# The first feed-forward of a six-layer Perceiver kernel: norm, weight turns and logits in one block, the shared expert's gate and up in one product, routing weights in halves

## The chip, the cores and the metric

One core of a Trainium2 chip runs the whole program: six layers, one launch, everything in f32 where it matters here. The metric is the device time of the launch in microseconds, the median of several executions. TensorE is the matrix engine, VectorE (DVE), ScalarE (ACT) and GpSimd (POOL) are the elementwise ones, SyncE (SP) issues the DMAs. SBUF has 128 partitions; PSUM has 8 banks of 128 x 512 f32, and TensorE writes only there.

## The reference, cut to what matters

The residual stream x has 4096 tokens (128 sequences of 32) of 128 features. The third of the six layers is a mixture of experts:

```
h      = layernorm(x)                                  # 4096 x 128
scores = sigmoid(h @ gate_w.T)                         # 16 experts
choice = scores + e_bias                               # 4 groups of 4 experts
         keep the 2 groups with the largest sum of their top two; of these take the 4 best experts
weight = scores[chosen] / (sum + 1e-20) * 2.5
g, u   = h @ gate_proj[e].T, h @ up_proj[e].T          # each expert 64 wide, all 16 are computed
y      = sum over e of weight[e] * (silu(g) * u) @ down_proj[e].T
y     += (silu(h @ shared_gate.T) * (h @ shared_up.T)) @ shared_down.T
x      = x + y
```

## The kernel before, in words

`perceiver_kernel` calls one function a layer; each opens a block in which every engine has its own program, and engines wait for each other by semaphores. A block ends when all engines have ended. The layer of this change is `phase_ffn0` (line 1478). x lies in SBUF as X, 32 tiles of 128 tokens, with the tile statistics made by the layer before.

**Norm.** `phase_norm` (line 165) is a block of its own. VectorE works out mean and 1/sqrt(variance) in a chain of small steps (lines 228 to 242), with one square root on ScalarE (line 256). Then come eight groups of four tiles: VectorE normalises three tiles (line 185), ScalarE one (line 189), TensorE turns the four (line 290) and ScalarE copies the result to XNT (line 268), the features on the partitions. SyncE loads the weights meanwhile (lines 1524 to 1531).

**Main block, start.** TensorE turns the router's weights and the first half of gate_proj, makes the 16 logits of each tile of tokens as 32 products whose moving operand has 16 columns (line 1603; in f32 each product is two instructions), then turns the other expert weights. ScalarE copies what was turned (line 1640) and makes the sigmoid (line 1651).

**Experts.** Two experts (2 x 64) fill the 128 rows of one product, so 8 units hold the 16 experts and the ninth the shared expert; the tokens go in 8 chunks of 512. Unit n of chunk c is `gates(c, a)`, n = 9c + a: a gate product (line 1580) and an up product (line 1583), each 128 x 512. ScalarE makes the Silu of the first (line 1645), VectorE multiplies it by the second into I (`product`, line 1678), GpSimd multiplies units 0 to 7 in place by the routing weights (line 1562), and `down(c)` (line 1592, 36 products of 128 columns, 72 instructions) adds up all nine units for four tiles. VectorE adds the result to X (`finished`, lines 1713 and 1717). The ninth unit's gate and up weights have 64 columns of use each; the other 64 are zeros (ST), so that it too is two full products. I has 4 slots of a chunk each, LAG is 3: TensorE makes units of chunks 0 to 3, then `down(0)`, units of chunk 4, `down(1)` and so on. The gate of unit n waits for Silu n - 2, its up for product n - 2.

**Routing weights.** VectorE finds the experts in a chain of dependent steps (lines 1694 to 1756), and `link` puts one `product()` between them whenever steps worth 4 units of weight have gone by (`room`; a step over all 16 experts counts 3, a small one 1). TensorE turns the result RW behind unit 29 (chunk 3, a = 2, line 1627), ScalarE copies it, SyncE writes it to DRAM (line 1539) and reads it back spread over the partitions as RWB, two reads of 1 MB a chunk (line 1546), each to 64 partitions; RWB has two buffers. GpSimd waits for both reads of a chunk before its first multiplication.

## Time and profile before

| | us |
|---|---|
| median of 3 runs | 2444.99 (2444.36 to 2445.66) |
| the profiled execution's own time | 2440.65 |
| its span, first to last instruction | 2438.7 |
| the layer of the change, in the span | 683.6 to 928.4 |
| TensorE busy in the span | 2083.5 (85%) |
| mean granted TensorE clock | 0.929 of full speed (2.4 GHz) |

One execution is profiled; times of instructions are counted from the start of its span. Busy time is not bound to matter: what counts is the chain of waits that sets the end of the stage. The rows come further down.

### The profile page before, as it was taken

How to read it: one execution, taken by the hardware profiler on the slowest of the kernel's cores; microseconds unless marked ns; L12 is line 12 of the kernel's file. 1: busy time of each engine (PE TensorE's matmuls, PEld its weight loads, DVE VectorE, ACT ScalarE, POOL GpSimd, SP SyncE). 2: the span in 40 equal slices, each digit the busy share in tenths (PEclk: the TensorE clock that was granted, in tenths of full speed). 3: DMA queues.
4: the chain of work that ended last, by engine and by line, in shares of the span. 5: the costliest groups of instructions: out<-in, count | busy, mean ns of one | idle time of the engine just before them, and what ended most of it. 6: DMA issues, size and time to landing. Idle time of an engine off the chain costs nothing. (4 is left out here: it accounts for less than half of the span.)

```text
span 2438.7 us, 77682 instructions
## 1 busy us (share of the span) xinstructions
PE 2083.5 (85%) x25732; PEld 1603.5 (66%) x25771; DVE 1634.8 (67%) x5601; ACT 1427.0 (59%) x3597; POOL 457.9 (19%) x1078
## 2 busy tenths in 40 slices
PE   5999999997988998999999999996556025699999
PEld 3878888875763677999999999995134013444454
DVE  4777777776755235877777787786989877631311
ACT  4888888886743115655555555555677577532322
POOL 2555555552300840000000000000000030000000
PEclk9999999998979999999999999997988555899999
DMA  3222222220012824565556556552000000100000
GB/s 90 81 76 79 75 77 73 77 70 4 0 29 60 164 58 114 120 129 122 106 121 131 109 109 131 120 109 70 0 1 0 0 2 3 49 5 5 9 4 13
DMA packets 266731, 158.07 MB, mean 65 GB/s; under 512 B 40560, under 2 KB 256512, under 8 KB 266240
## 3 DMA queue, kind: packets, MB, share of 16 engines
q1 hardware_dynamic: 266624, 156.65, 27.9%
q8 instruction: 66, 1.08, 0.2%
q14 instruction: 41, 0.34, 0.1%
HBM read 135.34 MB, written 21.23 MB: 64 GB/s over the span
## 5 line engine op out<-in xcount | busy, mean ns | idle before, releaser
L1195 ACT ACTIVATE c_PR<-c_PR,c_nmx 128x257 f32<-128x257 f32 x512 | 252.8, 496 | 69.8 <-DVE c_nmx L1242 69.8
L1238 DVE CUSTOM_DVE_ANT_0 c_PR<-c_b,c_MB 128x257 f32<-128x257 f32 x512 | 195.1, 424 | 125.4 <-PE c_b L1120 118.5
L684 ACT ACTIVATE a_PR<-a_SM,a_nmx 128x257 f32<-128x257 f32 x512 | 253.3, 499 | 4.1 <-POOL a_XL L459 3.6
L1131 PE MATMUL c_b<-c_PT,c_C 32*128 32x128 f32 x8192 | 238.8, 272 | 3.7 <-ACT c_QP L1188 2.1
L1131 PEld LDWEIGHTS c_b<-c_PT,c_C 32*128 32x128 f32 x8192 | 232.3, 187 | 7.9 <-issue 4.3
L1120 PE MATMUL c_b<-c_cT,c_QP 128*128 128x257 f32 x1024 | 230.5, 383 | 0.8 <-ACT c_QP L1188 0.8
L731 DVE CUSTOM_DVE_ANT_0 a_SM<-a_bs,a_MB 128x257 f32<-128x257 f32 x512 | 188.0, 423 | 60.4 <-PE a_bs L552 33.5
L1120 PEld LDWEIGHTS c_b<-c_cT,c_QP 128*128 128x128 f32 x1024 | 191.9, 190 | 31.2 <-issue 2.8
L1255 DVE STREAM_TRANSPOSE c_PT<-c_PR 128x256 f32<-128x256 f32 x512 | 181.4, 412 | 0.0
L1200 ACT ACTIVATE c_OT<-c_b 128x512 f32<-128x512 f32 x128 | 76.4, 597 | 169.0 <-PE c_b L1131 169.0
L1088 POOL TENSOR_TENSOR c_XL<-quarter,c_PR 128x16 f32<-128x16 f32 x128 | 27.6, 216 | 660.8 <-DVE c_PR L1250 660.8
L1250 DVE TENSOR_SCALAR c_PR<-c_PR,c_rden 128x257 f32<-128x257 f32 x512 | 146.3, 351 | 4.5
L2693 ACT ACTIVATE g_A<-g_b,g_S 128x512 f32<-128x512 f32 x64 | 44.0, 687 | 160.8 <-PE g_b L2614 160.7
L562 PE MATMUL a_bp<-ident,a_PR 128*128 128x128 f32 x1024 | 134.5, 274 | 1.7 <-ACT a_PR L684 1.4
L2813 DVE TENSOR_TENSOR g_YS<-g_b,g_s 128x512 f32<-128x512 f32 x8 | 5.5, 692 | 183.7 <-PE g_b L2668 183.7
L1150 PEld LDWEIGHTS c_b<-c_B,c_OT 128*128 128x128 f32 x1024 | 116.7, 192 | 16.1 <-DVE c_mx L1238 13.7
L2369 PE MATMUL d_bv<-d_WQ,d_HQ 128*128 128x512 bf16 x33 | 20.7, 633 | 124.8 <-PEq L2209 96.2
L1150 PE MATMUL c_b<-c_B,c_OT 128*128 128x128 f32 x1024 | 122.8, 278 | 4.6 <-DVE c_mx L1238 3.1
L1105 PE MATMUL c_b<-c_XNT,c_A 128*128 (+1 forms) x1024 | 122.1, 278 | 1.6 <-POOL c_VB L1094 1.6
L1188 ACT ACTIVATE c_QP<-c_b 128x512 f32<-128x512 f32 x128 | 75.7, 596 | 76.4 <-PE c_b L1105 76.4
L562 PEld LDWEIGHTS a_bp<-ident,a_PR 128*128 128x128 f32 x1024 | 117.0, 144 | 3.0 <-ACT a_PR L684 3.0
L1105 PEld LDWEIGHTS c_b<-c_XNT,c_A 128*128 128x128 f32 x1024 | 117.0, 192 | 2.5 <-POOL c_VB L1094 2.5
(496 smaller groups left out, 4804.1 us busy)
## 6 DMA issues: line engine op xcount, KB each, us to landing
c_C<-in_ctx_dram SPq DMA_DIRECT2D x512, 128.0 KB, 3.1
a_C<-in_ctx_dram SPq DMA_DIRECT2D x128, 128.0 KB, 2.1
ctxT_dram<-a_cT SPq DMA_DIRECT2D x128, 128.0 KB, 1.8
f_RWB<-f_rw_dram SPq DMA_DIRECT2D x16, 1024.0 KB, 13.5
c_cT<-ctxT_dram SPq DMA_DIRECT2D x128, 128.0 KB, 3.2
a_MK<-in_mask_Bx1xSxS_bk_dram SPq DMA_DIRECT2D x128, 32.1 KB, 1.9
X<-in_x_dram SPq DMA_DIRECT2D x4, 512.0 KB, 6.4
g_h<-in_L_ffn_h_w_dram SPq DMA_DIRECT2D x2, 1024.0 KB, 6.9
```

The lines of the kernel that those rows point to most:

```text
L562: last = nc.tensor.transpose(b_pt[pair][:, (2 * k + c) * P:(2 * k + c + 1) * P], PR[:, par, 2 * pair + k, c * P:(c + 1) * P], sh.ident[:, :])
L684: nc.scalar.activation(PR[:, 1 - par, hg, :], SM[:, 1 - par, hg, :], ACT.Exp, bias=nmx[:, 1 - par, hg:hg + 1], accum_out=den[:, 1 - par, h ...
L731: nc.vector.tensor_tensor_reduce(SM[:, par, hg, :], b_s[hg][:, 0:SK], MB[:, par, :], 1.0, NEG1, ALU.add, ALU.max, mx[:, par, hg:hg + 1]).t ...
L1105: last = nc.tensor.matmul(banks[:, c, i * P:(i + 1) * P], A[:, 4 * c + i, :], sh.XNT[:, ds(tile * P, P)], start=True, stop=True)
L1120: nc.tensor.matmul(banks[:, hg, 0:SK], QP[:, s.r, b, 4 * hg:4 * hg + 4, :], cT[:, buf, :], start=True, stop=True).then_inc(s_ps, 1)
L1131: last = nc.tensor.matmul(banks[:, h, 0:P], C[rows, b, kb, :], PT[rows, b, kb, :, :], start=(kb == 0), stop=(kb == NKB - 1), tile_position ...
L1150: nc.tensor.matmul(second[:, 0, 0:D], OT[:, par, h, :, :], BH[:, h, :], start=(h == 0), stop=False)
L1195: nc.scalar.activation(PR[:, b, hg, :], PR[:, b, hg, :], ACT.Exp, bias=nmx[:, b, hg:hg + 1], scale=SCALE, accum_out=den[:, b, hg:hg + 1]). ...
L1200: nc.scalar.activation(OT[:, par, :, b, :].rearrange("p (a h) q -> p h a q", h=4), banks[:, :, 0:P].rearrange("p h (a q) -> p h a q", a=4) ...
L1238: nc.vector.tensor_tensor_reduce(PR[:, b, hg, :], banks[:, hg, 0:SK], MB[:, :], 1.0, NEG1, ALU.add, ALU.max, mx[:, b, hg:hg + 1]).then_inc ...
L1250: nc.vector.tensor_scalar(PR[:, b, hg, :], PR[:, b, hg, :], rden[:, b, hg:hg + 1], None, ALU.mult).then_inc(n_ok, 1)
L1255: nc.vector.transpose(PT[:, b, :, hg, :], PR[:, b, hg, 0:LAST]).then_inc(t_ok, 1)
```

## The change

The norm's block goes: `phase_ffn0` has one block, and norm, weight turns and logits are interleaved by hand in each engine's order. The logits are made with the router's weights as the stationary operand, one product of 512 columns for each group of four tiles, and turned back in pieces of 16 rows into the same PSUM bank as before; half of the groups are copied by ScalarE, half by VectorE, and so are the turned expert weights. The shared expert's gate and up weights are turned together, so that one product gives the gate in partitions 0 to 63 and the up in 64 to 127; ScalarE writes the Silu to partitions 64 to 127, and the product and the down weights use these. The routing weights' turn stands behind unit 25 in place of 29, `room` begins at -8, `down(c)` follows the first two units of chunk c + 4 in place of the end of chunk c + 3, RW has another order, and each chunk's weights are read back in four DMAs of 512 KB, two for units 0 to 3 and two for units 4 to 7, for which GpSimd waits in turn.

```diff
--- before.py
+++ after.py
-        ST = sb("f_ST", [D, 2, P])
+        ST = sb("f_ST", [D, P])
...
-        sg, su = sb("f_sg", [FI, D]), sb("f_su", [FI, D])
-        sd = sb("f_sd", [P, FI])
+        sgu, sd = sb("f_sgu", [P, D]), sb("f_sd", [D, P])
...
-        RW = sb("f_RW", [P, 4, E_, NT // 4])
+        RW = sb("f_RW", [P, NC, 2, KE, 4])
...
+        LT = I[0:E_, LAG, 0:NC, :]
...
+            sp.dma_start(sgu[0:FI, :], sg_w).then_inc(s_in, 16)
+            sp.dma_start(sgu[FI:P, :], su_w).then_inc(s_in, 16)
...
-        phase_norm(nc, sh, "f_n_", loads, bk[0:2])
...
                 wait(sp, w_ok, KE * (c - 1))
-                rows = rw_dram[c // 2].rearrange("(a o) t k -> o a (t k)", o=2)
-                for o in range(2):
-                    sp.dma_start(RWB[FI * o:FI * o + FI, c % 2, :, :],
-                                 bcast(rows[o, :, CT * (c % 2):CT * (c % 2) + CT], 0, FI)).then_inc(rwb_in[c % 2], 16)
+                for h in range(2):
+                    for o in range(2):
+                        first = 64 * (c % 2) + 32 * o + 16 * h
+                        rows = rw_dram[c // 2, first:first + 16, :].rearrange("p k -> (p k)")
+                        sp.dma_start(RWB[FI * o:FI * o + FI, c % 2, 4 * h:4 * h + 4, :].rearrange("p a k -> p (a k)"),
+                                     bcast(rows, 0, FI)).then_inc(rwb_in[c % 2][h], 16)
...
+            clear_retired(pool)
...
+            nc.gpsimd.memset(sd[:, 0:FI], 0.0).then_inc(sd0_ok, 1)
+            nc.gpsimd.memset(I[0:FI, :, KE, :], 0.0).then_inc(zero_ok, 1)
             for c in range(NC):
-                pool.wait_ge(rwb_in[c % 2], 32 * (c // 2 + 1))
                 for a in range(KE):
+                    if a % 4 == 0:
+                        pool.wait_ge(rwb_in[c % 2][a // 4], 32 * (c // 2 + 1))
                     pool.wait_ge(i_ok, NA * c + a + 1)
                     nc.gpsimd.tensor_tensor(I[:, c % (LAG + 1), a, :], I[:, c % (LAG + 1), a, :], RWB[:, c % 2, a, :],
...
+            def rows(g):
+                pe.wait_ge(normed_v, g + 1)
+                pe.wait_ge(normed_a, g + 1)
+                wait(pe, xt_ev, g - 1)
+                for r in range(4):
+                    last = nc.tensor.transpose(tp[g % 2][:, r * P:(r + 1) * P], xn[:, g % 2, r, :], sh.ident[:, :])
+                last.then_inc(turned, 1)
+
+            def logits(g):
+                pe.wait_ge(xt_ev, g + 1)
+                wait(pe, lt_a if g % 2 else lt_v, g // 2)
+                nc.tensor.matmul(b_y[g % 2][0:E_, :], gateT[:, :], sh.XNT[:, g * CT:(g + 1) * CT],
+                                 start=True, stop=True).then_inc(lt_ps, 1)
+
+            def back(g):
+                pe.wait_ge(lt_a if g % 2 else lt_v, g // 2 + 1)
+                for r in range(4):
+                    t = 4 * g + r
+                    last = nc.tensor.transpose(b_l[:, t * E_:(t + 1) * E_], LT[:, g, r * P:(r + 1) * P],
+                                               sh.ident[0:E_, 0:E_])
+                return last
...
+                if a == 1:
+                    wait(pe, i_ok, n - 1)
+                nc.tensor.matmul(b_g[n % 2][:, :], GT[:, a * P:(a + 1) * P] if a < KE else ST[:, :], x,
                                  start=True, stop=True).then_inc(g_ps, 1)
-                wait(pe, i_ok, n - 1)
-                nc.tensor.matmul(b_u[n % 2][:, :], UT[:, a * P:(a + 1) * P] if a < KE else ST[:, 1, :], x,
-                                 start=True, stop=True).then_inc(u_ps, 1)
...
+            weights(b_t, [gw[:, :]], tw_ps)
+            rows(0)
+            pe.wait_ge(g_in, 16)
+            weights(bk[2], [gp[:, a, :] for a in range(4)], tw_ps)
+            rows(1)
+            pe.wait_ge(tw_a, 1)
+            logits(0)
+            pe.wait_ge(u_in, 16)
+            weights(bk[3], [up[:, a, :] for a in range(4)], tw_ps)
+            rows(2)
+            logits(1)
+            back(0)
+            weights(b_t, [gp[:, 4 + a, :] for a in range(4)], tw_ps)
+            rows(3)
+            logits(2)
+            back(1)
+            pe.wait_ge(tw_v, 1)
+            weights(bk[2], [up[:, 4 + a, :] for a in range(4)], tw_ps)
+            rows(4)
+            logits(3)
+            back(2)
             pe.wait_ge(s_in, 32)
-            turn(b_t, [sg[:, :], su[:, :]])
-            pe.wait_ge(t_ev, 5)
-            for c in range(NC + LAG):
-                if c < NC:
-                    for a in range(NA):
-                        if c == 0 and a == KE:
-                            pe.wait_ge(t_ev, 6)
-                            pe.wait_ge(st0_ok, 1)
-                        gates(c, a)
-                        if c == 1 and a < 2:
-                            pe.wait_ge(d_in, 32)
-                            turn(b_y[a], down_weights(a))
-                        if c == 1 and a == 2:
-                            turn(b_t, [sd[:, :]])
-                        if c == LAG and a == 2:
-                            pe.wait_ge(rw_ok, 1)
-                            for q in range(4):
-                                last = nc.tensor.transpose(b_l[:, q * P:(q + 1) * P],
-                                                           RW[:, q, :, :].rearrange("p e t -> p (e t)"), sh.ident[:, :])
-                            last.then_inc(rw_ps, 1)
-                if c >= LAG:
-                    if c == LAG:
-                        pe.wait_ge(t_ev, 9)
-                        pe.wait_ge(dt0_ok, 1)
-                    down(c - LAG)
+            pe.wait_ge(tw_a, 2)
+            weights(bk[3], [sgu[:, :]], tw_ps)
+            rows(5)
+            logits(4)
+            back(3)
+            rows(6)
+            logits(5)
+            back(4)
+            rows(7)
+            logits(6)
+            back(5)
+            pe.wait_ge(tw_v, 3)
+            pe.wait_ge(xt_ev, 7)
+            gates(0, 0)
+            logits(7)
+            back(6)
+            pe.wait_ge(tw_a, 3)
+            gates(0, 1)
+            back(7).then_inc(l_ps, 1)
+            for c in range(NC):
+                for a in range(2 if c == 0 else 0, NA):
+                    gates(c, a)
+                    if c == 1 and a < 2:
+                        pe.wait_ge(d_in, 32)
+                        weights(b_y[a], [dn[:, 8 * a + 2 * k:8 * a + 2 * k + 2, :].rearrange("p a b -> p (a b)")
+                                         for k in range(4)], dn_ps)
+                    if c == 1 and a == 2:
+                        pe.wait_ge(sd0_ok, 1)
+                        weights(b_t, [sd[:, :]], dn_ps)
+                    if c == LAG - 1 and a == KE - 1:
+                        pe.wait_ge(rw_ok, 1)
+                        for q in range(4):
+                            last = nc.tensor.transpose(b_l[:, q * P:(q + 1) * P],
+                                                       RW[:, 2 * q:2 * q + 2, :, :, :].rearrange("p c o a t -> p (c o a t)"),
+                                                       sh.ident[:, :])
+                        last.then_inc(rw_ps, 1)
+                    if c > LAG and a == 1:
+                        if c == LAG + 1:
+                            pe.wait_ge(dn_ev, 3)
+                            pe.wait_ge(zero_ok, 1)
+                        down(c - LAG - 1)
+            for c in range(NC - LAG - 1, NC):
+                down(c)
...
+                if n % NA < KE:
+                    nc.scalar.activation(SG[:, n % 2, :], b_g[n % 2][:, :], ACT.Silu).then_inc(g_ok, 1)
+                else:
+                    nc.scalar.activation(SG[FI:P, n % 2, :], b_g[n % 2][0:FI, :], ACT.Silu).then_inc(g_ok, 1)
...
+            nc.scalar.activation(warm[:, 0:1], sh.ident[:, 0:1], ACT.Sqrt)
+            act.wait_ge(var_ok, 1)
+            nc.scalar.activation(rstd, var, ACT.Sqrt).then_inc(std, 1)
+            nc.scalar.activation(warm[:, 1:2], sh.ident[:, 0:1], ACT.Sigmoid)
+            weights(0, gateT[:, :], b_t[:, 0:E_])
+            act.wait_ge(ready, 1)
+            normalised(0)
+            normalised(1)
+            copied(0)
+            weights(2, UT[:, 0:512], bk[3][:, :])
+            normalised(2)
+            copied(1)
+            normalised(3)
+            copied(2)
+            logits(1)
+            normalised(4)
+            copied(3)
+            normalised(5)
+            copied(4)
+            logits(3)
+            weights(5, ST[:, :], bk[3][:, 0:P])
+            normalised(6)
+            copied(5)
+            normalised(7)
+            copied(6)
+            logits(5)
+            copied(7)
+            logits(7)
...
-                if n == NA * LAG + 2:
+                    down_weights(2, DT[:, KE, :], b_t[:, 0:P])
+                if n == NA * LAG - 2:
...
-            n = room = made = 0
+            n = made = 0
+            room = -8
...
+            normalised(0)
+            normalised(1)
+            weights(1, GT[:, 0:512], bk[2][:, :])
+            logits(0)
+            normalised(2)
+            normalised(3)
+            weights(3, GT[:, 512:FE], b_t[:, :])
+            logits(2)
+            normalised(4)
+            weights(4, UT[:, 512:FE], bk[2][:, :])
+            normalised(5)
+            logits(4)
+            normalised(6)
+            normalised(7)
+            logits(6)
...
+            for o in range(2):
+                last = nc.vector.tensor_tensor(
+                    RW[:, :, o, :, :].rearrange("p c a t -> p c t a"),
+                    SEL[:, :, :].rearrange("p (c t) (a o) -> p c t a o", t=4, o=2)[:, :, :, :, o],
+                    bcast(tot[:, 1, :].rearrange("p (c t) -> p c t", t=4), 3, KE), ALU.mult)
+            last.then_inc(rw_ok, 1)
+            while made < NA * (LAG + 1):
                 product()
-            for c in range(LAG, NC + LAG):
-                while made < min(NA * (c + 1), NA * NC):
+            for c in range(LAG + 1, NC):
+                while made < NA * c + 2:
                     product()
-                finished(c - LAG)
+                finished(c - LAG - 1)
+                while made < NA * (c + 1):
+                    product()
+            for c in range(NC - LAG - 1, NC):
+                finished(c)
```

(`weights` in TensorE's program is the old `turn` with the semaphore as an argument; the norm's small steps on VectorE are those of `phase_norm`, and `normalised`, `copied` and `logits` on the other two engines wait for the turn or product, then normalise a tile or copy a bank.)

## Rows read from the trace of the kernel before

**Rows 1.** Timeline, 683 to 718: start us, us, engine, line, count [idle before]
```profile
687.28 1.83 DVE L185 TENSOR_SCALAR f_n_xn<-X,f_n_small 128x128 f32 x6 [0.29 <-issue]
688.25 2.03 PE L290 MATMUL f_b<-ident,f_n_xn 128*128 128x128 f32 x8 [6.19 <-DVE f_n_xn L185]
...
699.94 13.84 PE L1603 MATMUL f_b<-f_gateT,f_XNT 128*128 128x16 f32 x64 [0.28 <-ACT f_gateT L1640]
713.82 0.60 ACT L1651 ACTIVATE f_S<-f_b 128x512 f32<-128x512 f32 x1 [13.44 <-PE f_b L1603]
717.11 1.12 PE L1580 MATMUL f_b<-f_XNT,f_GT 128*128 128x512 f32 x2 [0.31 <-ACT f_UT L1640]
717.24 1.28 ACT L1656 ACT_TABLE_LOAD   x1
```
**Rows 2.** Windows: stretch, PE PEld DVE ACT POOL busy, clock, DMA share, GB/s
```profile
686.50:688.00 1.50, 0.00 (x0) 0.00 (x0) 1.14 (x6) 0.90 (x2) 0.00 (x0) 0.50 1.16 335
688.00:698.00 10.00, 8.25 (x32) 5.73 (x32) 6.48 (x22) 7.08 (x14) 0.00 (x0) 0.50 0.53 95
700.00:713.50 13.50, 13.50 (x64) 13.50 (x65) 0.00 (x0) 0.38 (x1) 0.00 (x0) 0.50 0.00 0
716.50:718.00 1.50, 1.19 (x4) 0.62 (x5) 0.00 (x0) 1.48 (x3) 0.00 (x0) 0.95 0.00 0
784.50:786.00 1.50, 0.00 (x0) 0.00 (x0) 0.00 (x0) 0.00 (x0) 0.00 (x0) 0.64 0.99 199
850.00:870.00 20.00, 20.00 (x85) 11.87 (x84) 7.07 (x13) 4.78 (x8) 14.36 (x13) 1.00 1.02 190
938.00:940.00 2.00, 2.00 (x23) 1.49 (x21) 0.36 (x1) 1.23 (x3) 0.00 (x0) 0.87 0.04 8
```
**Rows 3.** Timeline of VectorE, the routing chain
```profile
714.52 0.69 DVE L1694 TENSOR_TENSOR f_C<-f_S,f_eb 128x512 f32<-128x512 f32 x1 [18.27 <-ACT f_S L1651]
...
719.25 0.69 DVE L1678 TENSOR_TENSOR f_I<-f_SG,f_b 128x512 f32<-128x512 f32 x1 [3.62 <-ACT f_SG L1645]
...
755.92 1.09 DVE L1756 TENSOR_TENSOR f_RW<-f_SEL,f_tot 128x512 f32<-128x512 f32 x1
```
**Rows 4.** Timeline of TensorE, the routing weights' turn and the first down product
```profile
770.56 0.60 PE L1627 MATMUL f_b<-ident,f_RW 128*128 128x128 f32 x4
...
780.44 1.02 PE L1583 MATMUL f_b<-f_XNT,f_ST 128*128 128x512 f32 x2
798.61 9.89 PE L1592 MATMUL f_b<-f_DT,f_I 128*128 128x128 f32 x72 [17.15 <-POOL f_I L1562]
808.33 1.02 PE L1580 MATMUL f_b<-f_XNT,f_GT 128*128 128x512 f32 x2
809.19 1.02 PE L1583 MATMUL f_b<-f_XNT,f_UT 128*128 128x512 f32 x2
```
**Rows 5.** Timelines of SyncE and GpSimd; the reads of RWB: ns min/median/max
```profile
771.82 0.37 SPq L1539 DMA_DIRECT2D f_rw_dram<-f_TM  x1
774.11 85.17 SPq L1546 DMA_DIRECT2D f_RWB<-f_rw_dram  x16
...
L1546 SPq DMA_DIRECT2D f_RWB<-f_rw_dram x16: 573/636/2115, 774.1 to 858.6; - x16
...
788.55 9.80 POOL L1562 TENSOR_TENSOR f_I<-f_I,f_RWB 128x512 f32<-128x512 f32 x8 [89.11 <-DMA f_RWB<-f_rw_dram]
...
863.63 9.85 POOL L1562 TENSOR_TENSOR f_I<-f_I,f_RWB 128x512 f32<-128x512 f32 x8 [5.64 <-DMA f_RWB<-f_rw_dram]
```
**Rows 6.** Timeline of TensorE, the last four down products
```profile
894.25 32.32 PE L1592 MATMUL f_b<-f_DT,f_I 128*128 128x128 f32 x288
```
**Rows 7.** DMA issues, 680 to 900: KB, us to landing (issued at 683.98)
```profile
f_gp<-in_L_ffn_gate_proj_dram SPq DMA_DIRECT2D x1, 512.0 KB, 4.2
```
**Rows 8.** Timeline of TensorE, the next stage's first turns
```profile
932.53 1.97 PE L848 MATMUL c_b<-ident,c_wq 128*128 128x128 f32 x8 [5.96 <-DMA c_wq<-in_L_xattn_W_Q_dram]
```
**Rows 9.** Timeline of GpSimd, a memset of 256 columns
```profile
953.01 0.31 POOL L1094 MEMSET c_VB<- 64x256 f32 x1
```

More of the change, by code:

```diff
@@ L1515, in phase_ffn0 @@
[L1515 to L1517 removed]
+        rw_dram = nc.dram_tensor("f_rw_dram", (4, P, P), F32, kind="Internal").ap()
+        total, mean, diff, dsq, msq, var, rstd, half, shift = (small[:, i, :] for i in range(9))
+        gw_in, g_in, u_in, s_in, d_in, e_in = (sem("f_" + n) for n in ("gw_in", "g_in", "u_in", "s_in", "d_in", "e_in"))
@@ L1566, in _, with weights @@
         def _(pe):
-            def turn(bank, srcs):
+            def weights(bank, srcs, done):
                 for a, src in enumerate(srcs):
```

147 lines of the change are left out of this document (86 added, 61 removed).

## The prediction

> **What bounds the kernel now.** I read the page first: the span is 2438.7 us and the change touches one stage of it, from 683.6 to 926.6 us, so only that stage's own chain counts. The timeline then cuts it into four stretches. (a) From 687.28, when VectorE begins to normalise, to 717.11, when the first expert product starts, TensorE turns the normalised rows, then makes 64 logit products in 13.8 us, then turns the expert weights [rows 1], at half clock [rows 2]. (b) From 714.5 to 757.0 VectorE works out the routing weights: C at 714.52, the last product at 755.92 plus 1.09 [rows 3]. It puts 20 expert products between these steps, and waits 3.62 us for the first. (c) The weights are turned on TensorE only at 770.56, behind unit 29 of the gate and up products; they go to DRAM at 771.82, the first copy back is issued at 774.11, GpSimd starts at 788.55 [rows 4, 5]. TensorE has nothing left from 781.5 (780.44 plus 1.02) until the first down product at 798.61. (d) From there TensorE never stops: the last four down products, 288 instructions, take 32.32 us to 926.57 [rows 6].
>
> So the end of the stage is: start of the first down product plus TensorE's work behind it. A 512-column product in f32 (two instructions) takes 0.86 us at full clock, 808.33 to 809.19 [rows 4]; a chunk of 9 units is 18 of them, 15.45 us; a down product of 72 instructions 32.32 / 4, 8.04 us start to start. 798.61 + 4 x 15.45 + 8 x 8.04 + 1.7 (the first down product took 808.33 - 798.61 = 9.7 us, its clock being low after the idle time) = 926.4, and the trace has 926.57.
>
> **What the change does to each term.** *Shared expert as one product.* 17 products a chunk, not 18: 17 x 0.858 = 14.59 us, 0.86 us saved a chunk. Scalar and vector work keep their widths along the free axis (512), so their times stand.
>
> *Down products two units into the chunk.* The first one now comes after 38 units, not 36, and what stands behind it is 4 x 14.59 - 2 x 1.72 + 64.3 = 119.2 us, against 126.1. The slots of I free as before; VectorE makes two products and then adds the chunk to X. The next gate and up pair waits about 0.1 us for the first of these; I cost it at nothing, hidden by the 0.86 us gate product in front of it.
>
> *Start, one block.* The vector steps up to 687.28 stay, and the square-root table loads beside them as it did. The first rows can be turned at 688.25 as now [rows 1]; the gate weights land 683.98 + 4.2 = 688.2 [rows 7]. TensorE then has, up to the first half of the up weights, 16 transposes at 0.215 us (8 took 1.97 us at 932.53 [rows 8]) and one logit product of 512 columns, 1.72 us at half clock (twice 0.86, an estimate): 5.1 us, to 693.4. Does the clock rise then? In the next stage, whose norm is mixed with weight turns in the same way, it rose between 938 and 940, some 6 us after its first transpose [rows 2, 8]. I take full clock from 693.4. Then 33 transposes x 0.108, 6 logit products x 0.86 and 24 small turns of 16 columns: for these the nearest rows are the 64 logit instructions, 0.215 us each at half clock [rows 1], and the down product's 0.112 at full [rows 6]. I take 0.112. Sum 3.6 + 5.15 + 2.7 = 11.4 us.
> To this come waits that the new orders make. ScalarE normalises its tile of group 2 behind the copy of the up weights, which waits for their turn: TensorE stands 1.4 us. VectorE copies logits 2 and 4 before it normalises groups 4 and 6 (a copy of 0.6 and three tiles of 0.3 us each, 6 in 1.83 [rows 1]): 0.8 and 1.25 us. So the first expert product starts at 693.4 + 11.4 + 3.5 = 708.4 (bounds: 705 with no waits, 719.8 at half clock), 8.7 us sooner than 717.11.
>
> *Routing chain.* The logits now end behind two expert units: 708.4 + 2 x 1.72 + 0.86 + 8 x 0.112 = 713.6. Sigmoid 713.8, C 714.5: **no sooner than now**. The chain itself was 42.5 us. The 3.62 us wait goes, since the first product is due after 12 weight units instead of 4; 18 products, not 20, stand in it (2 x 0.6 less); the last step becomes two of half the size (+0.1, between +0 and +1.1). End 757.0 - 3.6 - 1.2 + 0.1 = 752.3. The price is that TensorE stands about 4.4 us near 715, for the Silu table (1.28 us [rows 1]) and for the first product at 718.3. It costs nothing as long as VectorE's chain is the bound; nothing else queues behind it.
>
> *Turn of the weights.* It stands behind unit 25. TensorE can't be further, at the chain's end, than VectorE's products let it: up product 20 waits for product 18, done at 752.9. Then 0.86 + 5 x 1.72 us: turned from 762.4, **8.2 us sooner** than 770.56.
>
> *Halves.* Write issued 1.25 us after (771.82 - 770.56), first read 2.3 us later: 765.95. Now the first chunk's two reads take 14.4 us to GpSimd's start, then 8 multiplications 9.8 us [rows 5]. In halves the second half is there after the same 14.4 us, and only 4 multiplications (4.9 us) stand behind it, the first four being done beside the load: 780.35 + 4.9 + 0.26 = **785.5** for the first down product, 13.1 us sooner than 798.61. SP issues 32 reads instead of 16 at 0.64 us [rows 5], 2.5 us a chunk, beside transfers of about 12.5 us. TensorE comes there at 762.4 + 0.43 (four turns) + 0.86 + 14.59 + 3.43 = 781.7, so 3.8 us idle instead of 17.
>
> *Clock.* In the idle time after 781.5 the slice 784.5 to 786 has a mean clock of 0.64 [rows 2]: it fell in it. My idle time of 3.8 us is about as long as that took, and it may fall or not: cost 0 to 1.7 us, and I take 1.7.
>
> *Small things.* GpSimd clears the old semaphores and sets 2048 columns of I to zero: 8 x 0.31 us by the nearest row [rows 9], needed only at 785, so free. It runs beside VectorE's first norm steps; if it holds them up, by at most that 2.5 us.
>
> **Sum.** 785.5 + 119.2 + 1.7 = 906.4 against 926.4: 20 us less. The profiled execution took 2440.65 us, so 2420.6; the median of the runs shown is 4.3 us above it: **2425**. A difference under 0.2% (4.9 us) can hardly be told from none here.
>
> **Rivals.**
> *Cold start* (chance 0.12). The clock was at 0.50 through the whole of the old norm (688 to 698), though TensorE was busy for 82% of it, and through the 64 logit products (700 to 713.5) with TensorE always busy; it rose only behind the weight turns, in 716.5 to 718 [rows 2]. If it stays there, 11.4 us become 22.8, the first product comes at 719.8 and the chain starts 11 us or more later: gain 5 to 10 us, 2437. For it: ScalarE and VectorE leave gaps. Against: the next stage's rise with the same mix.
>
> *Faster copies* (0.12). The reads now have lines of 8 KB in place of 2 KB, and alternate between the partition halves. Now they run at 190 GB/s with a DMA share of 1.02, while weight loads reach 335 [rows 2]. If they gain a third, 14.4 us become 10.8, and TensorE finds all ready when it comes at 781.7: gain 20 + 3.8 + 1.7 = 25.5, 2419. Against: both use the same source lines for 64 partitions, and that doesn't change.
>
> *Halves that cost* (0.10). The transfers are half as large, twice as many. If the per-chunk load goes from 12.5 us (863.63 - 788.55 over 6 chunks [rows 5]) to 15.6, the first down product is 3.6 us later: gain 16, 2429. If it goes over 18.4 us, GpSimd's stream sets the end: 765.95 + 8 x 18.4 + 4.9 + 8.3 = 926.4, and from there on the kernel is **slower**, by 8 us for each us more; at 20 us a chunk it is 2458 (chance of that 0.04, within the 0.10). Against: single loads of 512 KB are the quick ones above, so size isn't what limits the reads. The Trainium skill, "DMA: Bandwidth & Descriptors", section Bandwidth, advises batching to 1 MiB or more and has smaller transfers at a lower share of the peak; by its table a 512 KB transfer would run at roughly four fifths of the 1 MB rate (estimate), which is this rival's 15.6 us. The trace disagrees so far: 335 GB/s for 512 KB, 190 for 1 MB.
>
> *The early weights don't come early* (0.06). The idle time near 715 lets the clock fall, units 2 to 5 run at 3.4 us, and VectorE's chain waits for them: up to 5 us more, gain 15, 2430.
>
> **Numbers.** The forecast's own case has 0.60, with 2420 to 2428 from its bounds (+3 for a stretched last step and GpSimd's zeros, -5 for no waits and no clock loss). To hold 8 in 10 the range goes down to the faster copies, 2418, and up towards the cold start, 2436. Faster by over 0.2%: all but the slow half of the cold start and the slow loads: 0.92; within 0.2% 0.04; slower 0.04.
>
> **What would show it.** Right: first expert product near 708, C near 714.5, turn of the weights near 762, first down product near 785, chunk period 22.6 us in place of 23.5, stage end near 906. The first four multiplications of chunk 0 should start about 6 us before the second four. Wrong: half clock beyond 700, a chunk load over 15 us, or a down product that waits for GpSimd after the first.

## The result and the profile after

| | before | after |
|---|---|---|
| median | 2444.68 us (2442.03 to 2445.66, 4 runs) | 2422.57 us (2419.85 to 2422.83, 4 runs) |
| ratio, with its 95% interval | | 0.9907 (0.9894 to 0.992) |
| profiled execution, its span | 2440.65, 2438.7 | 2419.85, 2418.1 |
| the layer (the stage), from its first weight load to the next layer's | 244.86 | 227.44 |

The kernel is 22.1 us faster by the medians. The two profiled spans differ by 20.6 us, of which 17.4 lie in the layer; the other 3.2 come from layers that the change does not touch, and are spread between executions. Everything below is about the 17.4.

The timeline of TensorE, after, answers to [rows 1, 4, 6]: start us, us, engine, line, count, idle before.
```profile
689.00 1.12 PE L1582 MATMUL f_b<-ident,f_xn 128*128 128x128 f32 x4 [3.97 <-DVE f_xn L1773]
...
694.72 0.63 PE L1582 MATMUL f_b<-ident,f_xn 128*128 128x128 f32 x4 [1.11 <-DVE f_xn L1773]
695.27 1.03 PE L1588 MATMUL f_b<-f_XNT,f_gateT 128*16 128x512 f32 x2
696.24 0.42 PE L1595 MATMUL f_b<-ident,f_I 16*128 16x16 f32 x4
696.58 0.66 PE L1574 MATMUL f_b<-ident,f_gp 128*128 128x128 f32 x4
...
709.13 1.12 PE L1605 MATMUL f_b<-f_XNT,f_GT 128*128 128x512 f32 x2
...
714.27 0.42 PE L1595 MATMUL f_b<-ident,f_I 16*128 16x16 f32 x4
717.38 1.12 PE L1605 MATMUL f_b<-f_XNT,f_GT 128*128 128x512 f32 x2 [2.69 <-ACT f_SG L1714]
720.09 2.08 PE L1609 MATMUL f_b<-f_XNT,f_UT 128*128 128x512 f32 x2 [1.58 <-DVE f_I L1799]
...
764.61 0.60 PE L1678 MATMUL f_b<-ident,f_RW 128*128 128x128 f32 x4
...
786.62 9.90 PE L1618 MATMUL f_b<-f_DT,f_I 128*128 128x128 f32 x72 [2.49 <-POOL f_I L1566]
796.36 1.02 PE L1605 MATMUL f_b<-f_XNT,f_GT 128*128 128x512 f32 x2
797.36 1.13 PE L1609 MATMUL f_b<-f_XNT,f_UT 128*128 128x512 f32 x2
...
834.11 8.20 PE L1618 MATMUL f_b<-f_DT,f_I 128*128 128x128 f32 x72
...
857.01 8.20 PE L1618 MATMUL f_b<-f_DT,f_I 128*128 128x128 f32 x72
...
876.45 32.32 PE L1618 MATMUL f_b<-f_DT,f_I 128*128 128x128 f32 x288
```
The first expert product starts at 709.13 and the weights are turned at 764.61, 6 us sooner than in [rows 4]. The wait for GpSimd before the first down product is 2.49 us in place of 17.15. Two down products stand 22.90 us apart.

The timeline of VectorE, after, answers to [rows 3]:
```profile
685.76 0.19 DVE L1854 SCALAR_TENSOR_TENSOR f_small<-f_small 128x32 f32<-128x32 f32 x1
685.99 1.73 DVE L1855 TENSOR_SCALAR f_small<-f_small 128x32 f32<-128x32 f32 x1
...
715.42 0.69 DVE L1817 TENSOR_TENSOR f_C<-f_S,f_eb 128x512 f32<-128x512 f32 x1 [5.85 <-ACT f_S L1751]
...
751.66 0.69 DVE L1801 TENSOR_TENSOR f_I<-f_SG,f_b 64x512 f32<-64x512 f32 x1
...
753.21 1.08 DVE L1913 TENSOR_TENSOR f_RW<-f_SEL,f_tot 128x256 f32<-128x256 f32 x2
```
The routing chain takes 38.87 us, from 715.42 to 754.29, against 42.5. At its head, line 1855 takes 1.73 us where its neighbours of the same width take 0.19.

The timelines of GpSimd and SyncE, after, answer to [rows 5]:
```profile
685.89 1.80 POOL L1560 MEMSET f_I<- 64x2048 f32 x1
775.38 4.95 POOL L1566 TENSOR_TENSOR f_I<-f_I,f_RWB 128x512 f32<-128x512 f32 x4 [87.69 <-DMA f_RWB<-f_rw_dram]
781.43 54.00 POOL L1566 TENSOR_TENSOR f_I<-f_I,f_RWB 128x512 f32<-128x512 f32 x44 [1.10 <-DMA f_RWB<-f_rw_dram]
...
765.87 0.37 SPq L1542 DMA_DIRECT2D f_rw_dram<-f_TM  x1
768.17 70.13 SPq L1550 DMA_DIRECT2D f_RWB<-f_rw_dram  x32
```
The first half of chunk 0 is multiplied from 775.38, 6.05 us before the second. After that GpSimd makes 44 multiplications without a wait for a load.

Windows, after, as in [rows 2]:
```profile
692.00:693.50 1.50, 1.50 (x6) 0.42 (x4) 0.45 (x1) 0.00 (x0) 0.00 (x0) 0.92 0.00 0
693.50:708.00 14.50, 11.59 (x65) 5.74 (x65) 7.49 (x23) 8.24 (x18) 0.00 (x0) 1.00 0.00 0
719.40:722.60 3.20, 2.52 (x3) 1.17 (x4) 2.99 (x12) 0.60 (x1) 0.00 (x0) 0.52 0.00 0
788.00:791.00 3.00, 3.00 (x16) 3.00 (x16) 0.00 (x0) 0.00 (x0) 3.00 (x3) 0.50 0.95 199
800.00:830.00 30.00, 30.00 (x124) 17.57 (x123) 10.23 (x18) 7.76 (x13) 30.00 (x25) 1.00 1.02 218
```
TensorE's clock rises to 2.4 GHz just behind 692, falls to 1.2 GHz once near 720 and once more inside the first down product. The copies now run at 218 GB/s, against 190.

### The profile page after: what moved, and what is told of

Read it like the earlier page. It is cut to its first block and busy times, and to the rows that moved or that the text cites. A ratio compares the mean times of both kernels' runs of the same rounds, so it can differ in the third digit from the quotient of the medians.

```text
span 2418.1 us, 77577 instructions
## 1 busy us (share of the span) xinstructions
PE 2085.1 (86%) x25738; PEld 1586.2 (66%) x25738; DVE 1639.1 (68%) x5609; ACT 1426.7 (59%) x3599; POOL 459.2 (19%) x1078
## 3 DMA queue, kind: packets, MB, share of 16 engines
q8 instruction: 66, 1.08, 0.2%
## 5 line engine op out<-in xcount | busy, mean ns | idle before, releaser
L2533 PE MATMUL d_bv<-d_WQ,d_HQ 128*128 128x512 bf16 x64 | 33.1, 621 | 112.0 <-PEq L2373 96.0
```

## The experiments

"Stage" is the time from the layer's first weight load to the next layer's; the changed kernel has 227.44. "Turn" and "first down product" are counted from the same start: 81.40 and 103.41. Each kernel had one execution profiled, so that a difference of some tenths of a microsecond between two rows may be chance; the rows marked "again" show how far one kernel repeats. Times of the layer in us, C being the start of the routing chain on VectorE:

| kernel | stage | first expert product | C | turn | first down product |
|---|---|---|---|---|---|
| before | 244.86 | 33.52 | 30.93 | 86.97 | 115.02 |
| before, again (b_again) | 248.09 | 32.87 | 30.29 | 88.66 | 117.03 |
| after | 227.44 | 25.92 | 32.21 | 81.40 | 103.41 |
| after, again (c_again) | 227.62 | 25.94 | 32.23 | 81.44 | 103.59 |
| x1_whole | 233.25 | 26.46 | 32.76 | 82.22 | 109.29 |
| x2_lines | 229.74 | 26.45 | 32.74 | 82.19 | 105.74 |
| x3_extra | 230.28 | 26.52 | 32.81 | 82.29 | 104.50 |
| x4_turn20 | 223.16 | 25.97 | 32.27 | 72.89 | 100.83 |
| y7_turn29 | 232.73 | 26.12 | 32.41 | 87.74 | 108.94 |
| z1_oldstart | 225.11 | 32.73 | 29.98 | 81.95 | 102.71 |
| y1_zeros | 225.44 | 25.09 | 31.38 | 80.99 | 103.04 |
| y2_order | 224.93 | 23.09 | 29.38 | 78.83 | 100.90 |
| y3_room0 | 225.22 | 25.90 | 32.19 | 80.60 | 102.81 |
| y6_best | 215.00 | 23.79 | 24.59 | 64.73 | 92.67 |

Two things in these rows don't come from the edits. In x1_whole, x2_lines and x3_extra TensorE's clock rose 10.1 to 10.3 us into the layer, in the changed kernel 9.1: their first expert product is 0.5 us later and their turn 0.8 to 0.9, and these three are compared from the first read on. And the clock fell in the first down product of some executions and not of others, which is worth 1.6 us of the stage (last section).

**Halves (x1_whole).** Two reads of 1 MB a chunk, one wait.
```diff
-                for h in range(2):
-                    for o in range(2):
-                        first = 64 * (c % 2) + 32 * o + 16 * h
+                for o in range(2):
+                    first = 64 * (c % 2) + 32 * o
...
-                    if a % 4 == 0:
-                        pool.wait_ge(rwb_in[c % 2][a // 4], 32 * (c // 2 + 1))
+                    if a == 0:
+                        pool.wait_ge(rwb_in[c % 2][0], 32 * (c // 2 + 1))
```


> The changed kernel, with the routing weights of a chunk read back in two reads of 1 MB and waited for once, as before the change (the 8 KB lines stay). Theory 1 (halves let four of eight multiplications run beside the load): GpSimd starts when all has landed, 13.3 us after the first read, and needs 9.8 us; the first down product starts 4.9 us later than 786.6 and the stage (first weight load to the next stage's first load, 227.4 us in the changed kernel) is 4.9 us longer, 232.3. Theory 2 (twice as many, half as large reads are slower and eat the gain): whole reads land by more than 2 us sooner and the stage is longer by under 3 us. Theory 3 (the halves do nothing): 227.4.

The first theory's number: from the first read to the first down product it took 23.51 us against 18.45, 5.06 more, the four multiplications (4.95) that no longer run beside the load. The timelines of GpSimd and TensorE:
```profile
781.40 19.62 POOL L1565 TENSOR_TENSOR f_I<-f_I,f_RWB 128x512 f32<-128x512 f32 x16 [94.75 <-DMA f_RWB<-f_rw_dram]
803.84 9.86 POOL L1565 TENSOR_TENSOR f_I<-f_I,f_RWB 128x512 f32<-128x512 f32 x8 [2.83 <-DMA f_RWB<-f_rw_dram]
...
791.46 9.83 PE L1617 MATMUL f_b<-f_DT,f_I 128*128 128x128 f32 x72 [7.55 <-POOL f_I L1565]
```
GpSimd also waits for loads again between chunks, 2.83 us here, but TensorE isn't held by that: the second down product starts 24.52 us after the first, 24.59 in the changed kernel. The stage grew by 5.81 us; the 0.75 beyond the 5.06 lie ahead of the first read.

**Order of the weights in DRAM (x2_lines).** The halves stay; RW and its DRAM tensor have the old order, so that a line read is 2 KB in place of 8.
```diff
-        RW = sb("f_RW", [P, NC, 2, KE, 4])
+        RW = sb("f_RW", [P, 4, E_, NT // 4])
...
-                        first = 64 * (c % 2) + 32 * o + 16 * h
-                        rows = rw_dram[c // 2, first:first + 16, :].rearrange("p k -> (p k)")
+                        rows = rw_dram[c // 2].rearrange("(a o) t k -> o a (t k)", o=2)
...
+                                     bcast(rows[o, 4 * h:4 * h + 4, CT * (c % 2):CT * (c % 2) + CT], 0, FI)
```


> The changed kernel, still in halves, but with the order of the routing weights as before the change, so that a line read is 2 KB and not 8 KB. Theory 1 (the length of a line sets the rate of these reads): the rate falls from about 217 to about 200 GB/s, the second half of the first chunk lands 14.4 us after the first read in place of 13.3, and the stage is 1.1 us longer, 228.5; GpSimd waits for loads again in later chunks. Theory 2 (the 64 partitions of a read, not its lines, set the rate): 227.4 and the same rate.

Read to down product: 19.99 us, 1.54 more; GpSimd starts on the second half of chunk 0 14.81 us after the first read, in place of 13.26. The window of the same 30 us from 770, first of x2_lines:
```profile
770.00:800.00 30.00, 25.97 (x111) 16.46 (x109) 5.97 (x10) 5.96 (x10) 20.52 (x17) 0.94 0.91 198
```
then of the changed kernel:
```profile
770.00:800.00 30.00, 27.51 (x113) 17.02 (x112) 8.49 (x16) 6.56 (x11) 23.52 (x20) 0.94 1.03 219
```
So the new order is worth 1.5 us here, more than the 1.1 expected. My prediction had this as a rival and not as a term.

**The shared expert's product (x3_extra).** One 512-column product into the unused bank is put back into each ninth unit; nobody reads it.
```diff
+                else:
+                    wait(pe, i_ok, n - 1)
+                    nc.tensor.matmul(b_u[n % 2][:, :], ST[:, :], x, start=True, stop=True)
```


> The changed kernel with a second 512-column product in the ninth unit of every chunk, whose result nobody reads (the work that the one product for gate and up took away). Theory 1 (only what stands behind the first down product counts): 4 products of 0.86 us there, 3.4 us; of the four ahead of it, two fall where VectorE is the bound and two shorten TensorE's 2.5 us of waiting for GpSimd; stage 230.9. Theory 2 (TensorE is the bound all along): 8 x 0.86 = 6.9 us, 234.3. Theory 3 (product and Silu are the bound, not TensorE): under 1 us.

As the first theory said, the time from the end of the first down product to the end of the stage grew from 114.29 to 117.67 us: 3.38, four times 0.85. The stage grew by 2.84 only: the first down product came 1.09 us later, and in this execution the clock did not fall in it, 1.63 less.

**The turn's place (y7_turn29, x4_turn20).** Behind unit 29, where it was, and behind unit 20, with ScalarE's copy moved along. The first, then the second:
```diff
-                    if c == LAG - 1 and a == KE - 1:
+                    if c == LAG and a == 2:
...
-                if n == NA * LAG - 2:
+                if n == NA * LAG + 2:
```


> The changed kernel with the turn of the routing weights behind unit 29, its place before the change. Theory 1 (TensorE's order sets when the weights leave): the turn comes 0.86 + 3 x 1.72 = 6.0 us later, at 87.4 us of the stage, the first down product 6.0 us later at 109.4, and the stage is 6.0 us longer, 233.4 (with the clock's fall at the first down product, as in the changed kernel). Theory 2 (the sooner turn is worth nothing once the reads come in halves): under 2 us.

```diff
-                    if c == LAG - 1 and a == KE - 1:
+                    if c == LAG - 1 and a == 2:
...
-                if n == NA * LAG - 2:
+                if n == NA * (LAG - 1) + 2:
```


> The changed kernel with the turn of the routing weights behind unit 20 in place of 25. Theory 1 (the weights were ready at 754.3 and waited 10.3 us for their place in TensorE's order): the turn comes near 755.5, 9 us sooner; TensorE no longer waits for GpSimd before the first down product (2.5 us) and its clock doesn't fall there (1.7 us): stage 4.2 us shorter, 223.2. Theory 2 (the fall of the clock has to do with the down products, not with the wait): 2.5 us shorter, 224.9. Theory 3 (GpSimd and the loads, not TensorE's place, were last): no change.

The timeline of TensorE, of y7_turn29:
```profile
773.37 0.60 PE L1678 MATMUL f_b<-ident,f_RW 128*128 128x128 f32 x4
...
794.57 9.67 PE L1618 MATMUL f_b<-f_DT,f_I 128*128 128x128 f32 x72 [7.71 <-POOL f_I L1566]
```
and of x4_turn20:
```profile
756.60 0.60 PE L1678 MATMUL f_b<-ident,f_RW 128*128 128x128 f32 x4
...
784.54 8.20 PE L1618 MATMUL f_b<-f_DT,f_I 128*128 128x128 f32 x72
```
Four units later costs 5.3 us of the stage, where 6.0 were expected. The turn is 6.3 us later, but the first down product only 5.5, since from read to down product it took 17.39 us in place of 18.45. The four reads of chunk 0 show why. In the changed kernel the fourth landed 3.6 us behind the third, where its neighbours land 2.4 us apart, and in that time a 16 KB packet of the queue that the profile calls instruction held one of the 16 DMA engines for 1.3 us:
```profile
q8 instruction: 1, 0.02, 1.9%
```
(the DMA view of the changed kernel, 777.2 to 781.5: kind, packets, MB, share of the engines). In y7_turn29 that packet went 2.8 us before the first read, all gaps were 2.4 us, and GpSimd never waited for the second half. In each of the nine executions with the same reads in which such a packet went among the first ten reads, exactly one gap is 3.6 to 3.7 us, and the packet began in it or at most 1 us ahead of it. So at equal loads the place would be worth some 1.1 us more, about 6.4 (an estimate from these two executions).

Five units sooner gains 4.3: the turn comes 8.5 us sooner, but the wait had 2.49 us left to lose and the clock 1.7. Then TensorE comes to the first down product and finds everything ready, as the first theory said. The change left these 4 us where a constant in the program put them: the chain had ended at 754.29, and the weights waited 10.3 us for their place in TensorE's order.

**The new start (z1_oldstart).** The norm in its own block again, 64 logit instructions, all copies on ScalarE; everything behind it as changed.
```diff
+        phase_norm(nc, sh, "f_n_", loads, bk[0:2])
+        block = ctx.enter_context(nc.Block())
...
+            for t in range(NT):
+                last = nc.tensor.matmul(b_l[:, t * E_:(t + 1) * E_], sh.XNT[:, t * P:(t + 1) * P], gateT[:, :],
+                                        start=True, stop=True)
```


> The changed kernel with the old start: the norm in a block of its own, then 64 logit instructions of 16 columns and the weight turns, all copies on ScalarE; everything from the first expert unit on as changed. Theory 1 (only the time at which the logits are done counts, since VectorE's routing chain is the bound from there): C comes at 30.9 us of the stage as before the change, 1.3 us sooner than the changed kernel's 32.2, the first expert product 7.6 us later at 33.5, and the stage stays within 1.5 us of 227.4. Theory 2 (the sooner first expert product is what the new start brings): 7.6 us longer, 235.

The first expert product is 6.8 us later, C is 2.2 us sooner, and the turn comes only 0.55 us later: VectorE gets to its first product and waits 2.62 us for it. Its timeline, then GpSimd's:
```profile
720.28 0.69 DVE L1754 TENSOR_TENSOR f_I<-f_SG,f_b 128x512 f32<-128x512 f32 x1 [2.62 <-PE f_b L1611]
...
776.26 19.66 POOL L1568 TENSOR_TENSOR f_I<-f_I,f_RWB 128x512 f32<-128x512 f32 x16 [76.24 <-DMA f_RWB<-f_rw_dram]
```
So at the turn the largest part of the diff, the new start, is worth half a microsecond. This execution's stage is even 2.3 us shorter than the changed kernel's. Of that 1.6 is the clock, which did not fall in its first down product (8.11 us to the next product against 9.74), and 1.2 the reads: no instruction packet fell into those of chunk 0, GpSimd made 16 multiplications without a wait, and from read to down product it took 17.21 us. The half microsecond is one execution's: its clock was at 2.4 GHz from 693 to 699.5, in the old norm and just behind it, where the kernel before had 1.2 from 688 to 698 [rows 2], and at 1.2 again when the first units ran. A new start that is worth nothing, or 1 us, isn't excluded.

**What the start leaves (y1_zeros, y2_order, y3_room0).** GpSimd's zeros wait for the last normalised tile of VectorE; VectorE and ScalarE normalise before they copy logits and weights; `room` begins at 0.
```diff
+            pool.wait_ge(normed_v, 8)
             nc.gpsimd.memset(I[0:FI, :, KE, :], 0.0).then_inc(zero_ok, 1)
```


> The changed kernel with GpSimd's memset of 2048 columns of I moved behind the norm. Theory 1 (the memset holds a VectorE step of the norm: 1.73 us where it takes 0.19): normalising starts 1.5 us sooner, and so do the logits and the stage's end: 225.9. Theory 2 (TensorE's clock rises at the same time whatever it did 1.5 us sooner, and takes part of it back): 226.5 to 227. Theory 3 (the long step has another cause): 227.4.

```diff
-            weights(2, UT[:, 0:512], bk[3][:, :])
             normalised(2)
             copied(1)
             normalised(3)
+            weights(2, UT[:, 0:512], bk[3][:, :])
...
-            logits(0)
             normalised(2)
+            logits(0)
```
(and the same for logits 2 and 4)

> The changed kernel with normalising put ahead of the copies that wait for TensorE: on VectorE groups 2, 4 and 6 before logits 0, 2 and 4, on ScalarE groups 2 and 3 before the up weights. Theory 1 (the three waits of TensorE in the start, 1.1, 0.6 and 1.2 us, come from these copies): first expert product and C 2.9 us sooner, stage 224.5. Theory 2 (other copies are then last, ScalarE's above all): less than half of it.

```diff
-            room = -8
+            room = 0
```


> The changed kernel with room starting at 0 in place of -8, so that VectorE makes its first product after 4 units of weight. Theory 1 (with the turn behind unit 25 the number of products made in the chain counts, not its end): the chain ends 2 us later, but with 20 products made in place of 18, so the turn of the weights comes 1.4 us sooner (2 x 1.72 - 2.0), and the stage is 1.4 us shorter, 226.0; TensorE's clock doesn't fall near 720. Theory 2 (the end of the chain is what counts): 2 us longer, 229.4.

y1_zeros: line 1856, the step that line 1855 had been, is short again. Its timeline of VectorE:
```profile
686.90 0.19 DVE L1855 SCALAR_TENSOR_TENSOR f_small<-f_small 128x32 f32<-128x32 f32 x1
687.12 0.18 DVE L1856 TENSOR_SCALAR f_small<-f_small 128x32 f32<-128x32 f32 x1
```
The 1.5 us shrank to 0.83 at the first expert product and 0.41 at the turn, since the clock did not rise sooner with the work: by the windows of half a microsecond around it, it rose between 692 and 692.5 in the changed kernel and behind 693 in y1_zeros, whose layer begins 1.14 us later, so about 9 us into the layer in both. More of the turns ran at 1.2 GHz, as the second theory had it. The next 0.4 us went when the clock stayed down from 717.4 to 724, in the changed kernel from 719.7 to 722.9, and the first products came late. The stage's 225.44 looks like the first theory's 225.9, but that is luck: 1.6 of its 2.0 us are the clock, which did not fall in the first down product.

y2_order: the three waits of 1.11, 0.60 and 1.20 us are gone, and 2.83 us of that arrive at C and 2.57 at the turn. The same chain, moved, is moved to its end: that is what counts in the start, not when the first expert product runs.

y3_room0: a product is done sooner, the clock doesn't fall near 720 (1.00 over 716 to 724), and the turn comes 0.80 us sooner although the chain ends 1.86 later. So beginning at -8 made the chain shorter and fed TensorE later. The gain is smaller than the 1.4 us expected, since TensorE now waits 1.00 and 1.01 us near the chain's end and the clock falls there instead:
```profile
751.00:754.00 3.00, 3.00 (x5) 1.15 (x4) 2.77 (x5) 0.60 (x1) 0.00 (x0) 0.50 0.00 0
```
Of the 2.2 us by which its stage is shorter, 1.6 are again the clock in the first down product.

**All together (y6_best).** x4_turn20, y1_zeros and y2_order, and all logits ahead of the first two units, so that C need not wait for them:
```diff
             pe.wait_ge(tw_v, 3)
-            pe.wait_ge(xt_ev, 7)
-            gates(0, 0)
             logits(7)
             back(6)
+            back(7).then_inc(l_ps, 1)
             pe.wait_ge(tw_a, 3)
+            gates(0, 0)
             gates(0, 1)
-            back(7).then_inc(l_ps, 1)
```


> Turn behind unit 20, zeros behind the norm, normalising ahead of the copies, and all logits done ahead of the first two expert units, so that VectorE's routing chain starts sooner and the two units fall into TensorE's idle time of 4.4 us behind them. Theory 1 (the parts add up, since each brings the routing chain or the first down product forward): 223.2 of x4_turn20, less 2.5, less 0.4, less 3.1 for the chain's sooner start, 217.1; against the changed kernel 10.3 us, a ratio to the kernel before of 0.987. Theory 2 (the first product, Silu's table and the units themselves are late then): no more than 1 us from the last part, 219.5.

Its timeline of TensorE:
```profile
749.41 0.60 PE L1678 MATMUL f_b<-ident,f_RW 128*128 128x128 f32 x4
...
777.35 8.20 PE L1619 MATMUL f_b<-f_DT,f_I 128*128 128x128 f32 x72
```
Median 2410.18 us (2409.24 to 2410.87, 4 runs), ratio to before 0.9855 (0.984 to 0.9871); the changed kernel, timed beside it, has 2421.56 and 0.9901 (0.9887 to 0.9915). It beats both. The stage is 12.4 us shorter than the changed kernel's, where the parts add up to 10.3; its clock stayed at 2.4 GHz from 694 to 777 (1.00), and what else the 2.1 us are no run shows.

**The same kernels again (c_again, b_again).** No edit.

> The changed kernel once more, on the chip and against the kernel before of y6_best. Stage 227.4, or 225.8 where TensorE's clock doesn't fall at the first down product (it fell in two of four runs with a gap of 2.5 to 2.7 us before it). Theory 1 (that fall is chance): ratio to the kernel before 0.990 to 0.993. If y6_best's parts add up, it is 8 to 11 us slower than that one.

> The kernel before, once more, to see how far a stage's length repeats. If it does, the stage takes 244.9 us within 1 us and what is left of the span 2193.8 within 2 or 3 us. Theory 1 (the change does nothing outside its stage): the rest is in the range that the changed kernels show, 2190.7 to 2196.2. Theory 2 (later stages gain too): the rest is over 2196.

The changed kernel repeats within 0.2 us of the stage. The kernel before does not: b_again's stage is 3.2 us longer, where I expected 1 us at most, while the rest of its span is 2193.4 us, the 2193.8 of the first execution. Its timeline of VectorE, beside the 3.62 us of [rows 3]:
```profile
720.72 0.69 DVE L1678 TENSOR_TENSOR f_I<-f_SG,f_b 128x512 f32<-128x512 f32 x1 [5.36 <-PE f_b L1583]
```
and its windows:
```profile
716.00:720.00 4.00, 3.72 (x7) 1.80 (x7) 0.00 (x0) 2.85 (x5) 0.00 (x0) 0.50 0.00 0
```
Its clock rose near 721.6, 37.6 us into the layer, in [rows 2] 33.1 us into it, so the first units ran at 1.2 GHz and VectorE waited 1.74 us longer for the first product. The first down product took another 1.2 us more (10.93 to the next product, not 9.72). By the mean of the two executions of each kernel the stage fell from 246.5 to 227.5 by 18.9 us.

## Why the prediction was right, and where its terms were off

Predicted 2425.0 (2418 to 2436), measured 2422.57: the likeliest case came true. The sum was made for the profiled execution, 2420.6, which took 2419.85. But the stage itself was predicted 20 us shorter and is 17.4 shorter, so the sum was partly saved by the 3.2 us outside the stage, which no term stands for: that is luck. So is some of the median: I put it 4.3 us above the profiled execution, as before the change, and it is 2.7 above. Of the 22.1 us between the medians, some 19 are the stage's by the repeated profiles; the other 3 are no more than the runs of the kernel before differ among themselves (2442.03 to 2445.66).

- **Start.** From the stage's start, predicted 24.8 and measured 25.92. The clock rose just behind 692, not at 693.4; the cold start of the rivals came in none of the eleven executions that have the new start (a rise 9.0 to 10.3 us into the layer). The three waits came nearly as predicted, 1.11, 0.60 and 1.20 us for 1.4, 0.8 and 1.25. Three terms were too small. The step that GpSimd's zeros hold was named ("if it holds them up, by at most that 2.5 us") and costed at nothing; it is 1.5 us. A logit product of 512 columns takes 0.97 us to the next instruction, 695.27 to 696.24, not 0.86, 0.7 us for six. And a turn of a normalised tile takes 0.14 us to the next, not 0.108, 0.8 us for the 24 of them; the small turns, 0.086 us in place of 0.112, gave 0.6 back.
- **C "no sooner than now".** Right as a statement, and 1.3 us off in size: 32.21 from the start, predicted 30.9, in the kernel before 30.93. y6_best shows that this was mostly a choice of order: C can be at 24.59, of which y2_order alone has 2.8 us and y1_zeros 0.8.
- **The chain.** Predicted 37.8 us, measured 38.87. The wait of 3.62 us went, as predicted. The split last step cost nothing: 1.08 us for both, as one did in [rows 3]. The missing 1.1 us are in the timeline of VectorE. The shared expert's products have only 64 partitions (line 1801), and around each of the two in the chain 0.12 us are lost twice, ahead of it (0.72 us from the step before to the product, where others have 0.60 or 0.61) and behind it (0.72 for 0.60): 0.5 us. VectorE waits 0.40 us for TensorE after its clock had fallen near 720. And the two products that no longer stand in the chain saved 1.04 us, not 1.2: without one between them, two dependent steps start 0.33 us apart, with one the product starts 0.21 us after the first.
- **The early weights.** The rival with 0.06 came half true: TensorE stood near 715 and its clock fell (0.52 in 719.4 to 722.6). It cost 0.40 us of VectorE's chain, not 5, because only one product was late for it.
- **The turn.** Chain's end plus 10.3 us, predicted 10.1. Its time, 764.61 for 762.4, is late by the start and the chain. y7_turn29 prices the new place at 5.3 us.
- **Halves.** Read to the second half: 13.26 us, predicted 14.4. This term was mis-sized in our favour by 1.1 us: I kept the old rate, and the copies run at 218 GB/s. Without the instruction packet it would have been 1.2 us less still: the fourth read landed after 11.9 us in z1_oldstart and 12.1 in y7_turn29. The four multiplications off the path are 5.06 us (x1_whole), predicted 4.9.
- **First down product.** 786.62 for 785.5, idle before 2.49 us for 3.8, and its clock fell as assumed: 9.74 us for 8.04 plus 1.7.
- **Behind it.** 122.15 us (to 876.45 + 32.32) for 119.2 + 1.7. "I cost it at nothing" failed for the pair behind a down product: the up product does wait for VectorE's first product, as the prediction said, and is not hidden. From the waits of the changed kernel, 817 to 822 (PEld is the load of the stationary operand; us in all, times, longest):
```profile
PEld f_b L1609 <- DVE f_I L1799: 0.8, 1, 0.8
```
The gate product takes 1.00 us to the next, the up product 0.96, where both took 0.86 in the kernel before (831.82, 832.68, 833.54). Per chunk 22.90 us for 22.63, four times 0.27. The saved product itself is 3.38 us for 4 x 0.86 = 3.44.
- **Faster copies**, as a rival, had a third more rate. They got 15%. The Trainium skill, "SBUF — State Buffer", section "Door 1: The DMA port swizzle", states about 218 GB/s as what a transfer to partitions 0 to 63 can reach, half the ports of one to all 128. The trace agrees within a few per cent: 218 GB/s over 30 us, 225 over the 11 us from 770, and the single loads to 128 partitions in [rows 2] have 335. With that page of the Trainium skill this rival would have been smaller: by its figure 2 MB take 9.6 us per chunk (an estimate). The reads land 2.4 us apart, four of them a chunk.
- **Halves that cost** fell. In x1_whole, with reads of 1 MB and the same 8 KB lines, the 2 MB of chunk 0 reach GpSimd 13.45 us after the first read; in halves 13.26. Between 770 and 781 it moved 207 GB/s, the changed kernel 225. The rule of the Trainium skill, "DMA: Bandwidth & Descriptors", section Bandwidth, to batch to 1 MiB or more, which its table has for 128 partitions, doesn't hold for these reads.

Where the 17.4 us came from, each from the run that takes one part away: the turn's place 5.3, halves 5.1, longer lines 1.5, one product less in each of the four chunks behind the first down product 3.4, the new start 0.5. That is 15.8, or about 17 with the 6.4 for the turn's place at equal loads. The two units made ahead of the first down product take 3.4 us from behind it and cost 1.1 us in slower pairs; no run took them away alone, and the parts overlap where TensorE comes too late itself, so the sum isn't exact.

## What to carry to other kernels

Follow a result to the instruction that waits for it, and ask what stands before that instruction in its engine's order: here the weights lay ready for 10 us behind five units that could wait, and moving one `if` gained as much as splitting all transfers, while a rewritten start that ran 7 us ahead was worth 0.5 in the one execution that shows it. When a transfer feeds a chain of equal pieces, let the first pieces be released before the last have landed. And profile a kernel twice: the stage of the kernel before moved by 3.2 us with the times at which its clock rose, more than several of the terms in the sum, and nearly 3 us of an edit's price can be the clock (1.6) and one packet of instructions (1.2).

## What the runs showed of the hardware that was not expected

- A GpSimd memset, which reads nothing, holds a VectorE step of 32 columns until it ends: 1.73 us in place of 0.18 (y1_zeros). The step has one input from SBUF; the one before it, at 685.76 and with two, ran in 0.19 beside the shorter memset that GpSimd made at 685.80. The Trainium skill, "SBUF — State Buffer", section "SBUF: two separate sides", says of the port pair that the two engines share that it is an exclusive lock for the whole instruction, and that a VectorE step takes part in it in a two-port mode, or with two inputs, then only against a GpSimd operation that reads. The rows fit; that line 1855 ran in a two-port mode no row shows.
- After almost the same idle time the clock falls in the first down product or not: idle 2.49 us (after), 2.55 (y2_order) and 2.63 (c_again) with a fall, 9.74 us to the next product; 2.53 (y1_zeros) and 2.69 (y3_room0) without, 8.11. In the first three the fall came 1.1 to 1.5 us after work had begun again (the changed kernel has 1.2 GHz from 788 to 791, the product began at 786.62). These 1.6 us are chance where y1_zeros and y3_room0 are compared with the changed kernel. After 4.03 us (x2_lines), 7.55 (x1_whole) and 7.71 (y7_turn29) it fell, at the latest when the product began; after 1.00 (x3_extra), 1.24 (z1_oldstart) and no idle time at all (x4_turn20, y6_best) it did not, so there the missing fall may belong to the edit or to the quicker reads. But two waits of 1.00 and 1.01 us stand before the fall near 751 in y3_room0.
- One packet of 16 KB on the instruction queue takes a DMA engine for 1.3 us, and the read that it falls among lands 1.2 us late. In the changed kernel it goes 9.1 us behind the first read and delays the fourth, in x3_extra 6.3 us behind it and delays the third, in y7_turn29 ahead of all reads.
- A product over 64 partitions takes VectorE 0.69 us, as long as one over 128, so the halved shared expert saves VectorE nothing; it even adds 0.12 us ahead of it and 0.12 behind.
